# Mode products of a Fourier layer moved into the groups, half of the images at a time

## The reference

```
x = coords @ fc0_w + fc0_b                       # 3 -> 32 channels
for sw, cw, cb in four layers:
    x_ft = rfft2(x, norm='ortho')
    out  = einsum('bixy,ioxy->boxy', x_ft[:, :, :20, :20], sw)   # the mode products
    x1   = irfft2(out in the lowest 20x20 modes, zero elsewhere)
    x    = gelu(x1 + einsum('bchw,oc->bohw', x, cw) + cb)
x = gelu(x @ fc1_w + fc1_b);  return (x @ fc2_w + fc2_b)[..., 0]
```

## Time and profile before

| | us |
|---|---|
| median of 3 runs | 6326.73 (6322.72 to 6348.17) |
| the profiled execution | 6331.26 |
| its span, first to last instruction | 6329.5 |
| PE busy in it | 5549.8 (88%) |
| DVE, ACT, POOL busy | 2847.6, 2686.9, 1104.5 |

### The profile page before, as it was taken

The page is one execution under the profiler, slowest core; times in us unless marked ns, Lnnn a source line. Parts: engine busy times, 40 slices in busy tenths (PEclk is TensorE's granted clock), DMA queues, the critical chain, the costliest instruction groups (busy, mean ns, idle before and its releaser), DMA issues. The chain is left out here.

```text
span 6329.5 us, 274083 instructions
## 1 busy us (share of the span) xinstructions
PE 5549.8 (88%) x119214; PEld 4137.1 (65%) x119214; DVE 2847.6 (45%) x4430; ACT 2686.9 (42%) x5007; POOL 1104.5 (17%) x1049
## 2 busy tenths in 40 slices
PE   5999999999899899899999999999987687888888
PEld 4876678678768776777678767767774334343343
DVE  2443344344434443444344334434442666656573
ACT  2334433443353335333433443343334546455553
POOL 3220222032212222221222122203220000000000
PEclk9999999999999999999999999999998798888887
DMA  2111111111101110211111111111110000000000
GB/s 33 14 14 14 19 14 14 15 19 14 24 8 16 23 15 10 24 14 14 19 15 14 15 19 14 14 15 17 14 14 7 17 1 8 1 8 1 4 1 4
DMA packets 442993, 85.37 MB, mean 13 GB/s; under 512 B 437592, under 2 KB 437864, under 8 KB 441704
## 3 DMA queue, kind: packets, MB, share of 16 engines
q1 hardware_dynamic: 441832, 67.58, 8.5%
HBM read 63.33 MB, written 4.23 MB: 11 GB/s over the span
## 5 line engine op out<-in xcount | busy, mean ns | idle before, releaser
L217 POOL COPY x_T<-x_X 128x512 f32<-128x512 f32 x1024 | 1075.3, 1106 | 3624.8 <-ACTq L778 3453.9
L773 ACT ACTIVATE x_X<-ga 128x512 f32<-128x512 f32 x1280 | 752.0, 598 | 1108.9 <-PE ga L452 898.9
L629 DVE COPY x_X<-ev 128x512 f32<-128x512 f32 x640 | 438.3, 688 | 872.2 <-PE ev L471 833.9
L452 PEld LDWEIGHTS ga<-pw_rhs,x_X 64*64 64x64 f32 x32768 | 592.3, 135 | 280.8 <-issue 278.8
L629 DVE COPY V<-ev 104x512 f32<-104x512 f32 x608 | 411.3, 690 | 603.7 <-PE ev L418 444.9
L483 PEld LDWEIGHTS ev<-dft_consts,x_T 128*64 128x64 f32 x16384 | 577.6, 137 | 44.1 <-issue 44.0
L483 PE MATMUL ev<-dft_consts,x_T 128*64 128x80 f32 x16384 | 597.8, 233 | 7.1 <-POOL x_T L217 5.5
L452 PE MATMUL ga<-pw_rhs,x_X 64*64 64x64 f32 x32768 | 585.2, 218 | 3.3 <-issue 2.7
L444 PE MATMUL ga<-V,inv_w 40*64 40x512 f32 x4096 | 548.6, 603 | 29.2 <-ACT V L741 27.9
L629 DVE COPY Y<-ev 128x400 f32<-128x400 f32 (+1 forms) x768 | 463.1, 603 | 209.4 <-PE ev L483 166.2
L629 DVE COPY D<-ev 128x512 f32<-128x512 f32 x576 | 362.1, 684 | 337.9 <-PE ev L390 335.6
(11 more groups left out here) (200 smaller groups left out, 8372.1 us busy)
## 6 DMA issues: line engine op xcount, KB each, us to landing
mix_w<-in_sw SPq DMA_DIRECT2D x128, 400.0 KB, 7.9
coords<-in_coords SPq DMA_DIRECT2D x64, 96.0 KB, 2.1
maps<-Y SPq DMA_DIRECT2D x128, 16.0 KB
raw<-maps SPq DMA_DIRECT2D x8, 256.0 KB, 3.4
out<-out_t SPq DMA_DIRECT2D x8, 256.0 KB, 3.1
w<-in_w SPq DMA_DIRECT2D x3, 512.0 KB, 6.9
fc_rhs<-in_fc_w SPq DMA_DIRECT2D x32, 0.4 KB
dft_consts<-in_dft SPq DMA_DIRECT2D x1, 336.0 KB
```

The lines of the kernel that those rows point to most:

```text
L217: pool.tensor_copy(x_T[:, :, H * bc + h0:H * bc + h0 + 16].rearrange("p c (s n) -> p c s n", n=2), blocks.rearrange("p (s a n c) -> p a c ...
L452: last = pe.matmul(ps[HALF * bp:HALF * bp + HALF, HALF * s:HALF * s + HALF], x_X[r:r + HALF, g, col:col + HALF], pw_rhs[r:r + HALF, :], st ...
L629: dve.tensor_copy(dst, src).then_inc(ev_taken, 1)
L773: x_new = act.activation(blocks.rearrange("p (s a n) -> p s a n", s=8, a=2)[:, :, bc, :], ga[n % N_GA][:, :].rearrange("p (s n) -> p s n", ...
```

## The change

1. `mix_next` is gone. The products are made for half of the images at a time (`HC` = 8 images, 16 moving columns, `MIX_N` = 16), so there are twice as many. A half is two banks of the fifth slot (`mode_fifth`, 20 products each) and two bank pairs (`mode_pair`, 80 products each). They stand inside a group: the first half (groups 0 and 1) in group 2 of the layer that made it, the second (groups 2 and 3) in group 0 of the next layer.
2. In "mid" all four groups prepare the next: `turn_d((g + 1) % NG)`. In groups 0 and 2, where the products stand, the inverse H transform takes the all-row form (`inverse_h_rows`), in 1 and 3 the paired one. "first" prepares group 0 in its group 3 (two all-row steps, two paired).
3. A layer ends with `next_layer`: `inverse_w_and_pointwise(0)` of the next layer with `turn_d(1)` behind its first pair. The loop's jump stands behind it. New semaphore `pw_ready`: DVE tells that it has copied the next layer's pointwise weights.
4. The last stage projects the first two of four bank pairs of the next chunk before the jump. After the last chunk this is done once in vain, with a reload of coordinates by SP. Loads of `mix_w` wait for the second half's results in group 0.
5. Banks are numbered with offsets (`EV_OFF`, `GA_OFF`). DVE's and ACT's programs follow the new order: `mode_pair` on both, `mode_fifth` on ACT alone.

PE, end of the loop body "mid", before: the last mode products, the jump, and group 0's turn of S.

The core of the diff, on PE (new functions whole; DVE and ACT mirror the order):

```diff
-MIX_N = 2 * CHUNK
+HC = CHUNK // 2
+MIX_N = 2 * HC
@@ PE
-                def mix_next():
...
+                def mode_fifth(h, part):
+                    ps = ga_tile()
+                    passed()
+                    for k in range(MIX_K):
+                        at = MIX_K * part + k
+                        for jj in range(2):
+                            row = slice(HALF * jj, HALF * jj + HALF)
+                            last = pe.matmul(ps[row, MIX_N * k:MIX_N * k + MIX_N], mix_w[row, (KG - 1) * M + at, :],
+                                             S[row, 0, KG - 1, HC * h:HC * h + HC, 2 * at:2 * at + 2],
+                                             start=True, stop=True)
+                    last.then_inc(ga_ready, 1)
+                def mode_pair(h, p, to):
+                    pair = [ev_tile()]
...
+                    pair.append(ga_tile())
...
+                    for k in range(M):
+                        for jj, ps in enumerate(pair):
+                            row = slice(HALF * jj, HALF * jj + HALF)
+                            for cc in range(2):
+                                kg = 2 * p + (jj ^ cc)
+                                last = pe.matmul(ps[HALF * cc:HALF * cc + HALF, MIX_N * k:MIX_N * k + MIX_N],
+                                                 mix_w[row, kg * M + k, :],
+                                                 S[row, 0, kg, HC * h:HC * h + HC, 2 * k:2 * k + 2],
+                                                 start=True, stop=True)
...
+                def middle(g, d_at, half, to):
+                    written = n["ga"] - NB
+                    inverse = inverse_h_pair if half is None else inverse_h_rows
+                    for i in range(INV_T // 2):
+                        turn_x(g, range(2 * i, 2 * i + 2), written)
+                        if i < INV_T // 2 - 1:
+                            inverse(d_at, i)
+                        if half is not None and i == 0:
+                            modes_begin(to, MID_EV[g])
+                            mode_fifth(half, 0)
+                            mode_fifth(half, 1)
+                        if half is not None and i == 1:
+                            mode_pair(half, 0, to)
+                    y_at = forward_w(g)
+                    v_at = inverse(d_at, INV_T // 2 - 1)
+                    if half is not None:
+                        mode_pair(half, 1, to)
+                    forward_h(y_at)
+                    return v_at
+                def next_layer(v_at):
...
+                    pe.wait_ge(pw_ready, chunk * LAYERS + to + 1)
+                    passed()
+                    inverse_w_and_pointwise(0, (0, 0), lambda: turn_d(1))
@@ PE, last stage: group 0, and the end
+                    if g == 0:
+                        modes_begin(layer, 0)
+                        mode_fifth(1, 0)
+                        mode_fifth(1, 1)
...
+                    if g == 0:
+                        mode_pair(1, 0, layer)
                     fc1(1)
...
+                    if g == 0:
+                        mode_pair(1, 1, layer)
...
                     behind()
+                    ga0 = ga0 + GA_LAST
+                    n["ga"] = 0
+                    project_coords(0, range(NB // 4), ahead=1)
@@ PE, first stage: group 2 holds the first half of layer 0, group 3 prepares group 0
+                turn_x(NG - 1, range(TURN_X // 2), written)
+                modes_taken(2)
+                d_at = turn_d(0)
+                turn_x(NG - 1, range(TURN_X // 2, TURN_X), written)
+                y_at = forward_w(NG - 1)
+                for i in range(INV_T // 2):
+                    v_at = (inverse_h_rows if i < 2 else inverse_h_pair)(d_at, i)
+                forward_h(y_at)
+                next_layer(v_at)
```

## The result

The changed kernel takes 6581.4 us, the kernel before 6327.9 on the same chip: a ratio of 1.0392 (95% interval 1.0372 to 1.0412). It is some 250 us slower, where the prediction had 91 us faster and ended its range at 6310. Its profiled execution has a span of 6569.0 us.

A forecast was written before the change was run, and what follows sets the result against it. PE's work plus its standstills at layer changes was taken as the bound. -951 + 858 + 69 - 43 - 28 + 4 = -91 us turned 6331.3 into 6240, a median of 6236; range 6150 to 6310.

The forecast's parts named there:

- What goes: Between layers: all 32 stretches, 920.9 us, and the 29.9 us wait for Y ahead of the last forward H go, -951.
- rival 4: Layer change: the stretch stays, as PE needs V of group 0 and `pw_rhs` at once; no wait expected, no chance given.
- Mode products, bias, shape changes: New PE work in 64 halves: products at 58 ns a pass +445 us, bias products +29, changes of array shape +45.
- rival 3: Mode products: passes of 16 columns cost less than 58 ns, down to half, giving 6013 us; chance 0.07.
- Turn, inverse H, all-row: New PE work: turn of S for group 0 +75 us, its inverse H +150, all-row instead of paired in 48 groups +114.
- The jump: Loop's jump, now in dense work: 16 bare stands of 3.43 us, +55, and half-speed clock behind them, +14.
- Waits inside groups: PE's waits on DVE in groups 0 and 2 go, group 3 gains some: -1.8 us per middle layer, -43.
- At full clock, none of it hidden: All new PE work, +858 us, was priced at full clock and as fully exposed, since PE is the bound.
- rival 1: Mode products: the clock falls in them, about 1.7 us a piece, 192 pieces, up to 6562 us; chance 0.09.
- Chunk start: First four projections go ahead of the chunk's jump, leaving four behind it: 7 times -4.0 us, -28.
- DVE's and ACT's jumps, `load_mix`: DVE's jump before the turn of D, ACT's behind its last V, and SP's four weight loads: all hidden, costed at nothing.

The follow-up runs named there:

- a_paired: The changed kernel with the paired inverse H everywhere, its all-row steps undone: ratio 1.0813 to the kernel before.
- a_modes_half: The changed kernel with the mode products of every second k left out, the others moving 32 columns: ratio 0.9672 to the kernel before.
- b_double32: The kernel before with every mode product issued twice in its place, 32 columns each: ratio 1.0655 to the kernel before.
- a_cols32: The changed kernel with 32 moving columns instead of 16 in every mode product, the same eight images twice: ratio 1.0301 to the kernel before.
- b_lead: The kernel before with only the first four projections of the next chunk issued ahead of the chunk's jump: ratio 0.9981.
- b_nops2: The kernel before with 64 instructions that only count up a semaphore added to PE's stream in each forward W: ratio 1.1414.

## Why the prediction was wrong, by its steps

- **What goes** (-951): right. No stretch is left, and the wait for Y went; a wait of the same size at L475, 27.3 us, took its place, which the prediction expected not to come (its rival 4, "I expect no wait"). Its reason held for V; the wait is for S, since `next_layer` calls the inverse W with (0, 0) and so asks, at L468, for all of DVE's banks of the layer that ends.
- **Mode products, bias, shape changes** (+519): right as prices. A half is 2.44 + 2.89 + 2.56 = 7.9 us undisturbed, 64 of them 505. The choice of 58 ns for 16 columns was right, and rival 3 fell. The rule of the Trainium skill that was cited for it ("TensorE: Matmul & The Clock Gate", section LDWEIGHTS), 53 ns for 64 weight columns, agrees with these pieces at 16 and 32 columns.
- **Turn, inverse H, all-row** (+339): right in sum, as the table's work shows. Within it the all-row steps were priced too low: 15.6 us a chunk more than paired ones, and 21.0 by a_paired. The turn of S takes 2.33 us in all groups.
- **The jump** (+55 and +14): mis-sized. It stands 4.0 us, not 3.43, so 64; and 5.1 us at 0.53 follow, 2.4 lost where 0.85 was taken. Without jumps the clock's loss stayed, so the +14 was no term that could be taken away by itself.
- **Waits inside groups** (-43): this step failed. "The difference is PE waiting on DVE" misread its rows: PE was busy for 26.65 of the 27.02 us, so the 1.2 us were nearly all work (and its parts, 2x1.2 less 0.8, give 1.6 a layer, not 1.8). What waits the groups had ended for the most part without a releaser:

```profile
PE ev L418 <- issue: 23.3, 47, 0.9
...
PE ev L500 <- issue: 19.1, 30, 1.3
```

More work for PE did not end them, and new ones came. Idle time was to be 15.5 us a chunk and is 34.2. Of it 6.9 stand inside the pairs and 3.8 in the paired steps (3.4 before), mostly without a releaser, 8 at the jumps, and 3.4 at L475. a_modes_half and b_double32 tie those in the products to the number of instructions.
- **"At full clock, none of it hidden"**: this step failed, and by more. It is rival 1, which got 0.09. Its argument against ("the products themselves ran at 1.00", "a piece is 2.3 us between dense pieces") took the clock inside the piece for the clock that the piece leaves behind, and 32 columns for 16. The rival placed the falls in the products, and most come behind them: of 24.8 us a chunk lost while PE worked 4.8 were lost in mode products. That the few columns matter is shown by a_cols32; that many of the falls need a stand too, neither the rival nor the forecast had. Its price, 1.7 us a piece, holds at 1142.10; and 20.8 us a chunk are what 98 of the 192 pieces would cost, from 54 of which on the rival saw the gain gone.
- **Chunk start** (-28): right at its place, though b_lead, which has this step alone, gained only 12 us. From the last product of fc2 to `turn_x` it took 9.45 us and takes 5.40 now:

```profile
1318.80:1324.20 5.40, 4.11 (x20) 1.35 (x17) 0.75 (x1) 4.50 (x7) 3.21 (x4) 1.00 0.11 21
```

- **DVE's and ACT's jumps, `load_mix`** (nothing): no wait of PE names them.

## What to carry to other kernels

A gain that consists of idle and half-clock time is only had if the work that fills it keeps PE dense. Before work is cut into more and smaller products, count PE's instructions per microsecond against what its queue brings, and look at the clock behind such products, not inside them. A run that leaves half of the products out prices a doubling better than any row: here 46 to 56 us a chunk for work of 28.

## What the runs showed of the hardware

- With the same products and instructions 25.8, 14.9 and 7.1 us a chunk were lost to the clock at 16, 32 and 64 moving columns. At 16, 18 of 60 falls began 5.2 us or more behind PE's last stand; at 32 and 64 all 39 and 24 began in a stand or up to 2.5 us behind it.
- The mode products of 64x64 weights cost the same with 16 and 32 columns (2.56 and 2.57 us for the 160 records of a pair), but 3.08 with 64, in the run that repeats the columns.
- PE's instructions arrived in 16 KB packets of some 256, 19 of 20 no closer than 3.5 us, and 152 of PE's 202 stands without a releaser ended 2.3 to 3.0 us behind the start of one.
- An instruction that only counts up a semaphore, between two products, cost PE 0.11 us (b_nops2).
- At a loop's jump in dense work PE stood 4.0 us, and the clock fell at all 16 of them (the changed kernel).
